# An LSTM loop of 6250 steps: projections by three wide products a step, a body of 250 steps, a wait moved to VectorE, and edges laid on 128 partitions

## What is computed

```python
edge_index = jnp.stack([src, dst])            # 200000 edges, 6250 nodes, 256 features
x = x + gnn(layernorm(x), edge_weight, src, dst)
x = x + experts(layernorm(x)[None], ...)[0]
x = x + attention(layernorm(x), edge_index, ...)
x = x + lstm_block(layernorm(x)[None], ...)[0]

# in lstm_block, all float32, D = H = 256, 6250 steps:
x_proj = einsum('btd,gd->btg', x, W_ih) + b_ih + b_hh
def step(carry, xp):
    h, c = carry
    gates = xp + h @ W_hh.T
    i, f, g, o = split(gates, 4, axis=-1)
    c = sigmoid(f) * c + sigmoid(i) * tanh(g)
    h = sigmoid(o) * tanh(c)
    return (h, c), h
```

## Time and profile before

| | us |
|---|---|
| median of 3 runs | 28061.81 |
| lowest, highest | 28052.23, 28097.22 |
| the profiled execution | 28170.65 |
| its span, first to last instruction | 28168.7 |
| LSTM loop, share of that span | 10904 to 27993 |

### The profile page before, as it was taken

The page is one execution under the profiler, slowest core; times in us unless marked ns, Lnnn a source line. Parts: engine busy times, 40 slices in busy tenths (PEclk is TensorE's granted clock), DMA queues, the critical chain, the costliest instruction groups (busy, mean ns, idle before and its releaser), DMA issues. The chain is left out here.

```text
span 28168.7 us, 1333655 instructions
## 1 busy us (share of the span) xinstructions
PE 15516.8 (55%) x568992; PEld 11606.8 (41%) x569097; DVE 11412.2 (41%) x40890; ACT 7742.1 (27%) x39299; POOL 8112.6 (29%) x12875
## 2 busy tenths in 40 slices
PE   0000255668887775555555555555555555555555
PEld 0000133433346653444444444444444444444444
DVE  7000233357765553333333333333333333333334
ACT  0000000148861111333333333333333333333332
POOL 0777777327777760000000000000000000000000
PEclk9999877789998888999999999999999999999998
DMA  1000233200013341000000000000000000000000
GB/s 40 2 2 2 71 104 104 53 11 2 2 29 99 99 92 42 7 7 7 7 7 7 7 7 7 7 7 7 7 7 7 7 7 7 7 7 7 7 7 14
DMA packets 419954, 647.37 MB, mean 23 GB/s; under 512 B 271021, under 2 KB 298241, under 8 KB 412408
## 3 DMA queue, kind: packets, MB, share of 16 engines
q0 software_dynamic: 264912, 460.39, 7.1%
q1 hardware_dynamic: 148904, 98.78, 1.2%
HBM read 496.64 MB, written 60.32 MB: 20 GB/s over the span
## 5 line engine op out<-in xcount | busy, mean ns | idle before, releaser
L1129 POOL TENSOR_TENSOR ls_d<-ls_tf,ls_cell 128x2 f32<-128x2 f32 x6250 | 1234.9, 198 | 15862.3 <-ACT ls_tf L1171 15862.3
L1150 PE MATMUL banks<-ls_w,ls_ht 128*1 128x64 f32 x100000 | 2811.0, 222 | 3969.4 <-DVE ls_ht L1221 3759.2
L1156 PE MATMUL banks<-ls_w,ls_ht 128*2 128x64 f32 x200000 | 4446.8, 223 | 812.3 <-issue 807.6
L1143 PE MATMUL banks<-ls_xp,ident 128*1 128x64 f32 (+1 forms) x150000 | 3811.7, 224 | 1692.5 <-issue 1672.9
L1156 PEld LDWEIGHTS banks<-ls_w,ls_ht 128*2 128x2 f32 x200000 | 3333.6, 86 | 1162.3 <-issue 1160.8
L1150 PEld LDWEIGHTS banks<-ls_w,ls_ht 128*1 128x1 f32 x100000 | 1482.9, 83 | 5054.6 <-DVE ls_ht L1221 4800.4
L1143 PEld LDWEIGHTS banks<-ls_xp,ident 128*1 128x1 f32 (+1 forms) x150000 | 2732.5, 86 | 1925.8 <-issue 1904.8
L1211 DVE STREAM_TRANSPOSE ls_f_cols<-banks 128x64 f32<-128x64 f32 x6250 | 1562.1, 250 | 4690.4 <-PE banks L1150 4690.4
L1161 PE MATMUL banks<-ls_w,ls_ht 128*1 128x64 f32 x100000 | 2987.9, 222 | 640.0 <-issue 639.5
L417 PE MATMUL banks<-ag_rows,ag_pick 128*128 128x256 f32 x3328 | 1205.1, 525 | 3797.3 <-DMA ag_rows<-y_table,ag_idx 3764.0
L1171 ACT ACTIVATE ls_tf<-ls_f_cols 128x2 f32<-128x2 f32 x6250 | 1281.3, 205 | 6395.4 <-DVE ls_f_cols L1211 6395.4
(11 more groups left out here) (248 smaller groups left out, 18190.6 us busy)
## 6 DMA issues: line engine op xcount, KB each, us to landing
ag_rows<-y_table,ag_idx POOLq DMA_INDIRECT x1664, 2.7
mx_rows<-alpha_dst_table,mx_idx POOLq DMA_INDIRECT x1664, 2.3
at_rows<-wh_table,at_idx POOLq DMA_INDIRECT x1664, 2.8
rec_table<-st_rec,st_idx POOLq DMA_INDIRECT x1600, 2.6
projections<-xp_out SPq DMA_DIRECT2D x7, 3584.0 KB, 10.4
ls_xp<-projections SPq DMA_DIRECT2D x1000, 25.0 KB
rec_table<-zero POOLq DMA_DIRECT2D x5, 2496.0 KB, 28.9
rec_part<-rec_table SPq DMA_DIRECT2D x5, 2496.0 KB, 20.2
```

Source lines behind the costliest of these rows:

```text
L1143: x = nc.tensor.matmul(bank[32 * j:32 * j + m, 0:HD], pick, xp[:, b, j, :], start=True, stop=False, tile_position=(0, 32 * j))
L1150: m = nc.tensor.matmul(banks_f[s][32 * j:32 * j + 1, 0:HD], ht[:, v, c, 1:2], w[:, c, j, HD:2 * HD], start=False, stop=c == 1, tile_positi ...
L1156: m = nc.tensor.matmul(banks_ig[s][32 * j:32 * j + 2, 0:HD], ht[:, v, c, 1 - r:3 - r], w[:, c, j, lo:lo + HD], start=False, stop=(r, c) == ...
```

## The change

Three edits in the LSTM and one in the edge stages.

- **Projections.** `xp` holds a chunk of 5 steps as 40 partitions (8 for a step) by 128 values. A new constant tile `sel`, for each of the 5 steps a 128 by 128 matrix of zeros with eight ones, is the stationary operand of three products that each write all 128 rows of a bank (L1160 of the kernel after). The twelve narrow products go. Gate o comes out on row 32j+1 of its bank instead of 32j, so the o products have two weight columns.
- **Loop.** `LU` 25 to 5 and `CH` 2 to 50: the body is 250 steps, the loop has 25 turns, a chunk is 5 steps with one transfer, h goes to `HIST` every 5 steps from a ring of 10.
- **Wait.** ACT no longer waits for `f_mul` ahead of the tanh of i and g; DVE waits for it ahead of the scan.
- **Edges.** 128 partitions by 1562 columns, and a last column of 64 edges: 1563 columns. 78 turns of 20 scatters and three more.

```diff
-EP = 125
-EC = E // EP
+EP = P
+EF = E // P
+ER = E - EF * P
+EC = EF + 1
-LU = 25
-CH = 2
+LU = 5
+CH = 50
@@ stage_places
-            sp.dma_start(src[:, :], g["src"].rearrange("(p c) -> p c", p=EP)).then_inc(loaded, 16)
...
+            for tile, name in ((src, "src"), (dst, "dst"), (ew, "edge_weight")):
+                sp.dma_start(tile[:, 0:EF], g[name][0:EF * P].rearrange("(p c) -> p c", p=P)).then_inc(loaded, 16)
+                sp.dma_start(tile[0:ER, EF:EC], g[name][EF * P:E].rearrange("(p c) -> p c", c=1)).then_inc(loaded, 16)
+            link(nc.vector.memset(src[ER:P, EF:EC], -1))
...
@@ stage_scatter
-            with pool.Fori(0, EC // SU) as i:
+            with pool.Fori(0, FULL) as i:
...
+            for u in range(REST):
+                rows = P if FULL * SU + u < EF else ER
+                pool.wait_ge(g["scattered"][u], 16 * (1 + FULL * per))
+                own_wait(pool, g)
+                pool.indirect_dma_start(g["rec"][u], bass.IndirectOffsetOnAxis(ap=idx[0:rows, 0, u:u + 1], axis=0),
+                                        recs[0:rows, 0, u, :], None).then_inc(g["scattered"][u], 16)
@@ stage_lstm
-    R = 4
+    R = 8
-    xp = sb("ls_xp", [P, 2, 4, HD])
+    xp = sb("ls_xp", [P, 2, 2 * HD])
+    sel = sb("ls_sel", [P, LU, P])
-    ht = sb("ls_ht", [P, LU, 2, 3])
+    ht = sb("ls_ht", [P, 2 * LU, 2, 3])
-                for r in range(R):
-                    sp.dma_start(xp[32 * r:32 * r + LU, b, :, :],
-                                 rows.rearrange("u (j r n) -> u r j n", j=4, r=R)[:, r, :, :]).then_inc(xp_in[b], 16)
+                sp.dma_start(xp[0:LU * R, b, :], rows.rearrange("u (r n) -> (u r) n", r=R)).then_inc(xp_in[b], 16)
@@ tensor
-                    for bank, m, pick in ((banks_f[s], 1, g["ident"][:, 32 + u:33 + u]), (banks_ig[s], 2, g["ident"][:, u:u + 65:64]),
-                                          (banks_o[s], 1, g["ident"][:, 96 + u:97 + u])):
-                        for j in range(4):
-                            x = nc.tensor.matmul(bank[32 * j:32 * j + m, 0:HD], pick, xp[:, b, j, :], start=True, stop=False, tile_position=(0, 32 * j))
+                    for bank, lo in ((banks_f[s], HD), (banks_ig[s], 0), (banks_o[s], HD)):
+                        x = nc.tensor.matmul(bank[:, 0:HD], sel[:, u, :], xp[:, b, lo:lo + HD], start=True, stop=False)
-                            m = nc.tensor.matmul(banks_o[s][32 * j:32 * j + 1, 0:HD], ht[:, v, c, 1:2], w[:, c, j, 3 * HD:4 * HD],
+                            m = nc.tensor.matmul(banks_o[s][32 * j:32 * j + 2, 0:HD], ht[:, v, c, 0:2], w[:, c, j, 3 * HD:4 * HD],
@@ scalar
-                    act.wait_ge(f_mul, i * PER + (k + 1))
-                    nc.scalar.activation(to[:, :], to_cols[:, 0:33:32], ACT.Tanh)
+                    nc.scalar.activation(to[:, :], to_cols[:, 1:34:32], ACT.Tanh)
@@ vector
-                    if u == 0:
-                        dve.wait_ge(kept, i * CH + (k // LU + 1))
                     dve.wait_ge(gates_ready, i * (3 * PER) + (3 * k + 1))
                     vec.transpose(tf_cols[:, :], banks_f[s][:, 0:HD]).then_inc(turned, 1)
+                    if k % LU == 0:
+                        dve.wait_ge(kept, i * CH + (k // LU + 1))
...
+                    dve.wait_ge(f_mul, i * PER + (k + 1))
                     dve.wait_ge(ig_act, i * PER + (k + 1))
```

More of the change, by code:

```diff
@@ L238, in link @@
                 dve.wait_ge(step, n[0])
-            dve.wait_ge(loaded, 48)
+            link(nc.vector.memset(src[ER:P, EF:EC], -1))
+            link(nc.vector.memset(dst[ER:P, EF:EC], 0))
+            link(nc.vector.memset(ew[ER:P, EF:EC], 0.0))
+            link(nc.vector.memset(pos[:, EF:EC], 0.0))
+            dve.wait_ge(loaded, 96)
             link(nc.vector.tensor_single_scalar(hi_i[:, :], src[:, :], 7, ALU.arith_shift_right))
@@ L287, in stage_scatter @@
     per = SU // WAYS
+    FULL = EC // SU
+    REST = EC - FULL * SU
     recs = sb("st_rec", [EP, 2, SH, RF])
@@ L299, in _ @@
             stage_half(0, 1)
-            with act.Fori(0, EC // SU - 1) as i:
+            with act.Fori(0, FULL - 1) as i:
                 for h in range(2):
@@ L305, in _ @@
                     stage_half(i + 1, h)
+            for k in range(WAYS):
+                act.wait_ge(g["scattered"][k], (FULL - 1) * (16 * per) + 16 * (1 + per // 2))
+            nc.scalar.copy(recs[:, 0, 0:REST, :], g["REC"][:, FULL * SU:EC, :]).then_inc(staged, 1)
+            nc.scalar.copy(idx[:, 0, 0:REST], g["POS"][:, FULL * SU:EC]).then_inc(staged, 1)
         @block.gpsimd
         def _(pool):
-            with pool.Fori(0, EC // SU) as i:
+            with pool.Fori(0, FULL) as i:
                 for u in range(SU):
@@ L318, in _ @@
                                             recs[:, h, u % SH, :], None).then_inc(g["scattered"][k], 16)
+            pool.wait_ge(staged, FULL * 4 + 2)
+            for u in range(REST):
[4 more added lines that the diff above has]
+                                        recs[0:rows, 0, u, :], None).then_inc(g["scattered"][u], 16)
             for k in range(WAYS):
-                pool.wait_ge(g["scattered"][k], 16 * (1 + EC // WAYS))
+                pool.wait_ge(g["scattered"][k], 16 * (1 + FULL * per + (k < REST)))
 def stage_items(nc, sb, sem, g):
@@ L1123, in _ @@
         def _(pool):
-            pool.memset(free[:, :], 0.0).then_inc(kept, 1)
-            pool.wait_ge(zeroed, 4)
+            pool.memset(free[:, :], 0.0).then_inc(kept, 2)
+            pool.wait_ge(zeroed, 5)
             with pool.Fori(0, N // PER) as i:
@@ L1146, in _ @@
                     pe.wait_ge(h_ready, i * PER + (k + 1))
-                    v = (u - 1) % LU
+                    v = (k - 1) % (2 * LU)
                     for c in range(2):
@@ L1166, in _ @@
         def _(act):
-            act.wait_ge(zeroed, 4)
+            act.wait_ge(zeroed, 5)
             with act.Fori(0, N // PER) as i:
@@ L1180, in _ @@
                     if k % LU == LU - 1:
+                        v = k % (2 * LU) - (LU - 1)
                         act.wait_ge(h_ready, i * PER + (k + 2))
-                        nc.scalar.copy(g["HIST"][:, :, ds(i * PER + (k - LU + 1), LU)], ht[:, :, :, 1].rearrange("p u c -> p c u")).then_inc(kept, 1)
+                        nc.scalar.copy(g["HIST"][:, :, ds(i * PER + (k - LU + 1), LU)], ht[:, v:v + LU, :, 1].rearrange("p u c -> p c u")).then_inc(kept, 1)
         @block.vector
@@ L1186, in _ @@
             vec = nc.vector
-            vec.memset(xp[:, :, :, :], 0.0).then_inc(zeroed, 1)
-            vec.memset(ht[:, :, :, :], 0.0).then_inc(h_ready, 1)
-            for k in range(6):
-                vec.memset(g["ps"][k][:, 0:HD], 0.0)
+            vec.memset(xp[:, :, :], 0.0).then_inc(zeroed, 1)
+            vec.memset(sel[:, :, :], 0.0).then_inc(h_ready, 1)
             vec.memset(cell[:, :], 0.0)
             vec.memset(d[:, :, :], 0.0).then_inc(scanned, 1)
+            dve.wait_ge(h_ready, 1)
+            for j in range(4):
+                for r in range(2):
+                    m = vec.tensor_copy(sel[:, :, 32 * j + r], g["ident"][:, 2 * j + r:2 * j + r + R * (LU - 1) + 1:R])
+            m.then_inc(zeroed, 1)
+            vec.memset(ht[:, :, :, :], 0.0)
             dve.wait_ge(scanned, 1)
```

16 lines of the change are left out of this document (7 added, 9 removed).

## The result

The kernel after takes 30,740 us (30,466 to 31,003), the kernel before 28,065: a ratio of 1.092, interval 1.085 to 1.099. The forecast was 24,400 with a range to 25,350. It went the other way, by the rival that had a chance of 0.04.

A forecast was written before the change was run, and what follows sets the result against it. PE's instruction supply was taken to bound the loop. Loop 13,250 + 180 = 13,430 us against 17,089 (-3,660) and edge stages -45 gave 24,465 profiled, stated as 24,400 us; range 24,050 to 25,350.

The forecast's parts named there:

- the rival that had a chance of 0.04: LSTM loop: clock falls to 1.2 GHz throughout, PE sets steps of 3.17 us, total 31,000 us; chance 0.04.
- the clock's return behind an edge: Loop edges: the step after an edge was taken as only about 0.5 us slower, with PE at the slow pace.
- My two arguments against it: Against low clock: PE kept 1.00 in steps of 2.25 and over 3 us; 32 remaining narrow products come closer together.
- Supply as the bound before: LSTM loop of the kernel before: PE's instruction supply, one block in 3.7 us, sets steps of 2.605 us.
- The rival of a fixed cost per block: PE's instruction stream: each block border costs 0.49 us, 1,690 us would remain, total 26,000 us; chance 0.10.
- Three wide products hidden, at 0.11 us a pair: PE in each step: six wide load-product pairs take 0.67 us inside its wait for h, adding zero to the path.
- The moved wait, 0.145 us: Wait for f_mul moved from ACT to DVE ahead of the scan: chain shortens by 0.145 us to 2.11 us.
- The bound that I named: Moved wait's lower bound: 0 us gained if the wait on DVE costs at its end what it cost on ACT.
- 0.01 us for a late block: Loop step: 0.01 us added to the 2.11 us chain for unevenly arriving instruction blocks, giving 2.12 us.
- 24 edges for 124: Loop edges with a body of 250 steps: 24 x 7.5 = 180 us in place of 905 us.
- The edge stages, -45 us: Edge stages outside the LSTM loop: DVE passes -10, scatters -40, small loads and memsets +5, together -45 us.
- Total: Whole kernel: 24,465 us by the profiled execution's own time, stated as 24,400 us, ratio 0.87.

The follow-up runs named there:

- e1: Kernel after with its three wide projection products replaced by twelve narrow ones in every step, same 250-step body: 27,003 us, ratio 0.956.
- e2: Kernel after plus 32 unused narrow products of 256 columns at the head of each of the 25 turns: 24,631 us, ratio 0.872.
- e3: Kernel after with narrow projection products in the first 10 steps of each 250-step turn, wide ones in the other 240: 24,598 us, ratio 0.871.
- e8: e3 with DVE's two waits ahead of the scan swapped (ig_act, then f_mul): 25,228 us, ratio 0.873, in a later group of runs.
- e12: e8 with a longer body, CH = 250: 5 turns of 1250 steps; 24,923 us, ratio 0.864.
- e11: Kernel after with a wide product for gate o only, narrow ones for the other two banks, in every step: 26,738 us, ratio 0.927.
- e6: Kernel before with only the wait for f_mul moved from ACT to DVE: ratio 1.000.
- e9: e2 with its stretch of 32 narrow products ahead of each turn's 126th step instead of at its head: 28,226 us, ratio 0.978.

## Why the prediction was wrong

**The step that failed is taking the clock's return behind an edge as given**: the forecast priced the slow pace there at 0.5 us for one step, and gave 0.04 to the rival in which it stays. In 23 of 25 turns it stayed for the whole turn, 1.11 us a step over 250 steps. The rival had the right place (all wide pairs at 0.22 us, PE as the bound), the right price (3.17 us a step, measured 3.29; 31,000 us in all, measured 30,740) and a chance of 0.04. My two arguments against it were both from the kernel before, where every step had only narrow products, and both looked only at whether the clock would fall in mid-loop. The first of them rested on a window of 37 us and does not hold for the whole loop: inside the bodies of the kernel before the clock fell 48 times, for at most 6.8 us each, and came back each time. One such fall:

```profile
15640.00:15649.00 9.00, 4.96 (x287) 4.06 (x288) 3.65 (x18) 3.00 (x18) 0.79 (x4) 1.00 0.01 4
15650.00:15656.00 6.00, 4.89 (x177) 4.10 (x167) 1.95 (x10) 1.74 (x11) 0.40 (x2) 0.50 0.03 7
15657.00:15670.00 13.00, 7.66 (x453) 6.35 (x448) 5.24 (x25) 4.10 (x25) 0.99 (x5) 1.00 0.02 6
```

e1, with narrow products throughout, has 104 of them; e2, e3, e8 and e12, with wide ones and the clock up, have none (and hardly any of the stalls by the supply). So wide products did not pull the clock down in mid-turn; with them it did not come back from an edge. What I failed to ask is what happens behind an edge, where rows 4 had shown PE at the slow pace already. The kernel before came back from that within one or two steps, 124 times. I took the return as given, priced the step behind an edge at 0.5 us, and did not ask whether the changed step would return as well. The row stood there; the question that it called for was: is the slow pace a state that the new step can stay in? It can, as 23 turns show, and its price, 3.2 us of PE's work a step, stood in my own text. The chain at that level is shorter (2.79 us a step in e1), so PE becomes the bound there, and that makes the loss so large; that it is also why the clock stays down is not shown, and e11 speaks against it.

The other steps, by the runs in which the clock was up:

- **Supply as the bound before**: right. e6 (a shorter chain, no gain) and e1 (the long body with the old number of products: 2.6 us a step) are what it foretold. The queue gave a block in 3.70, 3.74 and 3.73 us with 177, 177 and 165 instructions a step (the kernel before, e1, e11). The rival of a fixed cost per block, which left 1,690 us, is out: e3 has 177 us of such waits. The "mostly hidden" of the Trainium skill ("Runtime: NRT & Kernel Launch", section "Instruction fetch mechanics") does not hold for this PE stream of 177 instructions in 2.25 us: e1's steps take 2.6. One reading was wrong, though nothing hangs on it: in rows 4 PE had loaded 15 of the 24 weights, not 24, when it stood still for 2.61 us.
- **Three wide products hidden, at 0.11 us a pair**: right at 2.4 GHz, (0.74 - 0.19) / 5 = 0.11, and PE waited 0.43 us for h.
- **The moved wait, 0.145 us**: half of it, 0.076, as undisturbed steps went from 2.255 to 2.179. The bound that I named (the wait on DVE costs something at its end) was what happened; e8 gets the missing 0.067 back with steps of 2.112, which is the 2.11 of the forecast.
- **0.01 us for a late block**: too little. In e8, where supply and chain lie closest, the wide steps average 2.140 against an undisturbed 2.113, so 0.027 (2.154 with the ten narrow steps of each turn).
- **24 edges for 124**: right in kind; an edge cost 8.9 us from h to h in e3, or 6.7 more than a step, where 7.5 were taken. The 9.07 us read from one edge of the kernel before are a little low: its 124 edges average 9.7.
- **The edge stages, -45 us**: mis-sized tenfold, 440 to 470 us. I had bounded a scatter of 128 rows from "costs what one of 125 does" to "grows with the rows", and left out that it could cost less, though the gather of 128 rows at 0.95 us stood beside it in rows 8. The scatter with 128 rows takes 0.96 us.
- **Total**: 28,170 - 17,089 + 13,952 - 440 = 24,593 for the profiled execution with the clock up; e3 measured 24,598, in a group whose kernel before took 185 us more, so part of this agreement is luck. With the clock up the forecast of 24,400 would have been about 0.8% low, and that closeness is luck too, since two misses partly cancel: the loop came out 520 us longer than its 13,430, the edge stages 395 us shorter than said.

**What stays open.** Why ten narrow steps or 32 narrow products are enough, while a turn of steps at 3.29 us with PE full is not; why turns 11 and 22 of the kernel after came up by themselves; and what it is about the wide products that keeps it down (PE being the bound is not enough, by e11). The runs show which stretches lifted the clock and which did not, and no more.

## What to carry to other kernels

When TensorE's clock falls at some place of a loop, ask of the changed step and not of the old one whether it gets out of there: cost it at the lower clock, and if it would be slow there, give that case real weight. The old step's quick return says nothing of the new one. Here ten steps with narrow products behind each such place were cheap insurance (250 steps in 6250, for 6,100 us); two were not always enough. In this loop, whose waits ended in "issue", a shorter chain bought nothing until the instructions were fewer; where you see such waits, count instructions first.

## What was not expected of the hardware

- A full PE is not a PE at full clock: a turn with PE busy for 817 of 817 us was granted 0.50, and the next turn of the same code 1.00. Either state lasted to the end of its turn. Nor is a full PE kept down: in e11 and e9 the clock rose out of it.
- The clock's level cost 1.11 us a step of 2.18, over half.
- An indirect scatter of 125 rows holds POOL for 1.18 us, one of 128 rows for 0.96 us.
- Of two waits ahead of DVE's scan, the one that is an instruction of its own made it start 0.07 us later when its event came last (e3 against e8).
